# Attention heads: softmax denominators partly summed by GpSimd, value products in column quarters and in pairs, results kept channel-major in SBUF

## The chip, the cores and the metric

The kernel runs on one core of a Trainium2 chip. Its time is the device time of one execution in microseconds (us), taken as the median of several executions. The engines are named as in the profile: PE (TensorE), DVE (VectorE), ACT (ScalarE), POOL (GpSimd), SP (SyncE, which here only issues DMAs).

## The reference, cut to what matters

Four images of 256 channels and 32 x 32 pixels pass through an attention over pixels, a group norm with eight attention heads, and a mixture of eight experts. The change lies in the heads:

```python
qkv = (h @ w_qkv + b_qkv).reshape(B, N, H, 3, d)        # B=4, N=1024, H=8, d=32
q, k, v = (qkv[..., 0, :], qkv[..., 1, :], qkv[..., 2, :])
scores = jnp.einsum('bnhd,bmhd->bhnm', q, k) * (1.0 / np.sqrt(d)).astype(x.dtype)
attn = jax.nn.softmax(scores, axis=-1)
vals = jnp.einsum('bhnm,bmhd->bnhd', attn, v).reshape(B, N, C)
out = vals @ w_proj + b_proj
return out + x
```

All values are float32. There are 32 heads in all (4 images by 8), each with 1024 queries n and 1024 keys m.

## The kernel before, in words

The program has four phases, each a block at whose end all engines meet: `conv_phase` (first attention, group norm, projections of q, k and v), `head_phase` (the 32 heads), `output_phase` (projection of the heads' values, residual, layer norm, routing) and `expert_phase` (39 tiles of 128 tokens). Every instruction order is written out by hand, and semaphores tie the engines together.

**A head.** `head(t, j)` in `head_phase` handles head 4t + j in eight blocks i of 128 keys. Operands lie in a ring of four slots (`SLOTS`), loaded by SP with seven DMAs per head (`Heads.load`, L198 and L199). In a block PE does:

- `scores` (L946): two matmuls of 512 query columns into one of two pairs of PSUM banks, `ps_e`. ACT then writes their exponentials to SBUF (L928) as `expd`, a ring of four tiles of 128 x 1024.
- `maxima` (L209): q k once more, for a head one or two ahead and the other way round, queries on the partitions. DVE reduces each half of 512 to a maximum per query (`block_max`, L215). The two halves of `ps_m` are single buffers: PE may write a half only after DVE has read what was there, by the semaphore `v_max`. The maxima are `LEAD` = 12 blocks ahead of the scores.
- `values` (L962): for the exponentials of two blocks earlier, four matmuls that go to the four groups of 32 columns of the array at once: v and a matrix of ones, each for two halves of 512 queries. So a bank `ps_o` collects, over eight blocks, 32 rows of values and 32 rows of the same denominator, for each half of the queries.

After four blocks of a head the previous head is ended: ACT copies its bank to `osum` (L919), PE transposes that by four (L954), DVE takes the reciprocal of 8 denominators per partition (L1010) and multiplies (L1014), and SP stores 128 x 8 x 32 values to `o_scr` in DRAM (L869).

The maxima of the next head are made ready once per head: `split_max` on DVE (L225, L227, L229: a minimum, a cast and a difference of 128 x 8), `max_turn` on PE (L235, waits for `split_max`), `next_rows` on ACT (L242) and `max_rows` on SP (L248), which puts them as two rows into the scores' operand. Before, `split_max` follows the fourth block's maxima and `max_turn` the fifth block's values.

**Around it.** The first `LEAD` blocks of maxima are done at the end of `conv_phase`, between its last pieces of work, as the table `HEAD_BLOCKS` says: (2, 2, 2, 1, 1, 1, 1, 1, 1). Pieces 4 to 7 are the projections of q and k (`heads_qk`, L606: eight matmul instructions each, then ACT L476 and DVE L763, the latter ahead of the reductions of the block that follows the piece). POOL loads the experts' second weights `w2` during the heads (L910). At the end of `head_phase` SP loads constants, the values of image 0 and the residual. In `output_phase`, per image, the values are loaded from `o_scr` (`vals_load`), transposed on PE (`turn_vals`, L138), copied by ACT (L1130) and projected in two halves (`project`, L146); DVE adds the residual (L1240) and goes on from there.

```python
for half in range(2):
    for kind, w in enumerate((vh[s][:, m, :], ones[:, :])):
        c = (2 * half + kind) * D
        mm = nc.tensor.matmul(ps_o[k][c:c + D, :], w, expd[:, m % RING, half * HALF:(half + 1) * HALF], ...)
```

## Time and profile before

| what | value |
|---|---|
| median of 3 runs | 1323.39 us (1320.49 to 1324.12) |
| the profiled execution | 1324.85 us |
| its span, first to last instruction | 1323.0 us |
| mean granted TensorE clock | 0.95 of full speed |
| head phase, by the timeline | about 355.8 to 909.5 us |
| output phase | about 910 to 1000 us |
| expert phase | about 1000 to 1323 us |

The span is what the trace covers; the execution's own time is 1.85 us longer. In the trace PEld is the loading of weights into the array, which overlaps PE's matmuls, and L numbers are lines of the kernel before. In the changed kernel the same lines stand two to some twenty lines further on.

### The profile page before, as it was taken

How to read it: one execution, taken by the hardware profiler on the slowest of the kernel's cores; microseconds unless marked ns; L12 is line 12 of the kernel's file. 1: busy time of each engine (PE TensorE's matmuls, PEld its weight loads, DVE VectorE, ACT ScalarE, POOL GpSimd, SP SyncE). 2: the span in 40 equal slices, each digit the busy share in tenths (PEclk: the TensorE clock that was granted, in tenths of full speed). 3: DMA queues.
4: the chain of work that ended last, by engine and by line, in shares of the span. 5: the costliest groups of instructions: out<-in, count | busy, mean ns of one | idle time of the engine just before them, and what ended most of it. 6: DMA issues, size and time to landing. Idle time of an engine off the chain costs nothing. (4 is left out here: it accounts for less than half of the span.)

```text
span 1323.0 us, 21162 instructions
## 1 busy us (share of the span) xinstructions
PE 1219.5 (92%) x6723; PEld 772.7 (58%) x6724; DVE 682.5 (52%) x1540; ACT 420.2 (32%) x465; POOL 207.6 (16%) x418
## 2 busy tenths in 40 slices
PE   6899999895999999999999999998971999999995
PEld 3677676663534444444443444434861899999995
DVE  3265455446666666666666666652862333333331
ACT  1312132220255555555555555553210111111110
POOL 0002030302000000000000000000054244434442
PEclk8899999795999999999999999998965999999998
DMA  6203353131532332323323322205636565656551
GB/s 196 56 2 118 132 171 128 64 127 64 201 102 53 90 83 76 96 64 96 93 63 90 83 55 64 64 9 158 216 140 159 169 207 188 210 185 211 194 199 64
DMA packets 97141, 156.78 MB, mean 119 GB/s; under 512 B 44848, under 2 KB 65264, under 8 KB 96464
## 3 DMA queue, kind: packets, MB, share of 16 engines
q1 hardware_dynamic: 86576, 121.81, 30.1%
q0 software_dynamic: 9712, 31.35, 7.4%
q10 hardware_dynamic: 816, 3.15, 0.7%
q8 instruction: 21, 0.34, 0.1%
q14 instruction: 16, 0.13, 0.0%
HBM read 108.77 MB, written 44.06 MB: 116 GB/s over the span
## 5 line engine op out<-in xcount | busy, mean ns | idle before, releaser
L215 DVE TENSOR_REDUCE s_nmax<-h_ps_m 128x1 f32<-128x512 f32 x488 | 314.4, 686 | 178.2 <-PE h_ps_m L209 177.7
L928 ACT ACTIVATE h_expd<-h_ps_e 128x1024 f32<-128x1024 f32 x256 | 261.9, 1024 | 237.4 <-PE h_ps_e L946 232.6
L962 PE MATMUL h_ps_o<-h_expd,h_ones 128*32 128x512 f32 x1024 | 270.7, 604 | 0.0
L962 PE MATMUL h_ps_o<-h_expd,s_vh 128*32 128x512 f32 x1024 | 270.7, 604 | 0.0
L1559 PEld LDWEIGHTS ps_h<-xs_c,lnt 128*128 128x128 f32 x1248 | 148.2, 195 | 4.8 <-issue 2.9
L1559 PE MATMUL ps_h<-xs_c,lnt 128*128 128x128 f32 x1248 | 148.6, 278 | 2.3 <-DVE xs_c L1511 2.3
L1569 PE MATMUL ps_y<-w,vals_t 128*128 x624 | 141.2, 379 | 0.6 <-DVE ys L1524 0.6
L578 PE MATMUL a_ps_v<-a_val,a_expd 128*128 128x257 f32 x512 | 120.0, 388 | 5.1 <-ACT a_expd L456 4.5
L1569 PEld LDWEIGHTS ps_y<-w,vals_t 128*128 128x128 f32 x624 | 115.5, 190 | 15.1 <-issue 1.0
L1600 ACT ACTIVATE vals_t<-ps_h 128x1024 f32<-128x1024 f32 x39 | 39.9, 1024 | 263.3 <-DVE ps_h L1504 263.3
L1504 DVE TENSOR_TENSOR ps_h<-ps_h,b_t 128x1024 f32<-128x1024 f32 x39 | 48.1, 1233 | 131.5 <-PE ps_h L1559 131.5
L578 PEld LDWEIGHTS a_ps_v<-a_val,a_expd 128*128 128x128 f32 x512 | 98.0, 193 | 25.1 <-ACT a_expd L456 6.5
L962 PEld LDWEIGHTS h_ps_o<-h_expd,s_vh 128*32 128x32 f32 x1024 | 38.8, 108 | 93.6 <-issue 93.3
L687 DVE TENSOR_REDUCE a_nmax<-a_ps_m 128x1 f32<-128x512 f32 x64 | 41.2, 685 | 67.8 <-PE a_ps_m L538 67.8
L910 POOL DMA_DIRECT2D w<-in_w x8 | 7.1, 888 | 384.5 <-PE h_ps_e L946 384.5
L416 POOL TENSOR_TENSOR a_res<-a_res,a_lnt 128x2048 f32<-128x2048 f32 x4 | 18.1, 4532 | 265.2 <-DVE a_lnt L121 265.2
L606 PE MATMUL a_ps_e<-a_h_c,a_w_qk 128*128 128x512 f32 x128 | 58.6, 609 | 0.3 <-ACT a_h_c L467 0.3
L1401 POOL TENSOR_TENSOR pause<-pause 128x1 f32<-128x1 f32 x156 | 30.3, 194 | 158.6 <-DVE ys L1524 133.1
L946 PE MATMUL h_ps_e<-s_stk3n,s_stk3m 98*128 98x512 f32 x128 | 46.4, 444 | 0.0
L946 PE MATMUL h_ps_e<-s_stk1n,s_stk1m 98*128 98x512 f32 x128 | 46.4, 443 | 0.0
L946 PE MATMUL h_ps_e<-s_stk0n,s_stk0m 98*128 98x512 f32 x128 | 46.3, 443 | 0.0
L946 PE MATMUL h_ps_e<-s_stk2n,s_stk2m 98*128 98x512 f32 x128 | 46.3, 443 | 0.0
(188 smaller groups left out, 1421.9 us busy)
## 6 DMA issues: line engine op xcount, KB each, us to landing
lnt<-in_w SPq DMA_DIRECT2D x39, 1024.0 KB, 4.8
qk_scr<-a_head_hi SPq DMA_DIRECT2D x16, 512.0 KB, 2.7
qk_scr<-a_head_lo SPq DMA_DIRECT2D x16, 512.0 KB, 3.6
w<-in_w POOLq DMA_DIRECT2D x8, 1024.0 KB, 6.1
xs<-xs_scr SPq DMA_DIRECT2D x39, 128.5 KB, 2.0
a_x_t<-in_x_t POOLq DMA_DIRECT2D x4, 1024.0 KB, 10.4
r_scr<-a_res POOLq DMA_DIRECT2D x4, 1024.0 KB, 6.0
v_scr<-res SPq DMA_DIRECT2D x4, 1024.0 KB, 3.9
```

What stands on the lines that cost most here:

```text
L215: self.nc.vector.tensor_reduce(self.nmax[k][:, nb, half:half + 1], ps_m[:, half, :], AX.X, ALU.max, negate=True).then_inc(self.v_max, 1)
L578: last = nc.tensor.matmul(ps_v[:, j % 2, 0:C + 1], expd[:, m, j * P:(j + 1) * P], val[b % 2][:, m, :], start=(m == 0), stop=(m == NB - 1))
L606: last = nc.tensor.matmul(ps_e[it % 2][:, half, :], w_qk1[:, t, it, :], h_c[:, t, half * HALF:(half + 1) * HALF], start=(t == 0), stop=(t ...
L687: nc.vector.tensor_reduce(nmax[b % 2][:, nb, half:half + 1], ps_m[:, half, :], AX.X, ALU.max, negate=True).then_inc(v_max, 1)
L928: nc.scalar.activation(expd[:, m % RING, :], flat(ps_e[m % 2]), ACT.Exp, scale=SCALE).then_inc(a_exp, 1)
L946: last = nc.tensor.matmul(ps_e[m % 2][:, half, :], m_st[:, m * P:(m + 1) * P], n_st[:, half * HALF:(half + 1) * HALF], start=True, stop=True)
L962: mm = nc.tensor.matmul(ps_o[k][c:c + D, :], w, expd[:, m % RING, half * HALF:(half + 1) * HALF], start=(m == 0), stop=(m == NB - 1))
L1401: nc.gpsimd.tensor_tensor(pause[:, n:n + 1], pause[:, 0:1], pause[:, 0:1], ALU.add)
L1504: nc.vector.tensor_tensor(blocks, blocks, b1_t[:, bass.ds(e, 1), :].rearrange("p o (k n) -> p (o k) n", n=1).to_broadcast([P, KC, P]), ALU ...
L1559: last = nc.tensor.matmul(ps_h[k][:, c // 4, c % 4 * P:(c % 4 + 1) * P], w1_now[k][:, t, c * P:(c + 1) * P], xs_c[:, t, :], start=(t == 0) ...
L1569: last = nc.tensor.matmul(ps_y[:, 0:C], hid_t[k][:, c, :], w2[:, bass.ds(e, 1), c, :].rearrange("p o n -> p (o n)"), start=(c == 0), stop= ...
L1600: nc.scalar.activation(hid_t[k].rearrange("p k n -> p (k n)"), flat(ps_h[k]), ACT.Gelu).then_inc(a_gelu, 1)
```

## The change

1. **Values by query quarters** (`values`): all four column groups now hold v, each for a quarter of 256 queries. One tile of exponentials takes four matmuls of 256 columns in place of four of 512.
2. **Denominators** (`sums`, `all_sums`): into the other half of the same bank, ones times exponentials, by quarters as well. For tiles 6 and 7 of a head it is done directly; tiles 0 to 5 (`ADDED` = 6) are first added up by POOL, with five additions of 128 x 1024 per head, and PE multiplies only their sum. So a head has 8 + 3 rounds of four 256-column matmuls.
3. **Pairs** (`head` on PE): scores and maxima of two blocks follow each other, then the values of two earlier tiles; the last two tiles and their sums come in the first pair of the next head (`tail`).
4. **End of a head**: no copy by ACT and no transposes. DVE takes the reciprocal of a 128 x 256 tile of PSUM and multiplies 128 x 256. SP moves the result with four DMAs of 32 rows each into `vals`, which stays in SBUF with channels on the partitions.
5. **Lead**: the maxima are 14 blocks ahead; the table of `conv_phase` becomes (2, 2, 2, 2, 2, 1, 1, 1, 1). `split_max` now follows the second block's maxima, `max_turn` stands at the end of the first pair, and the slot of the head two ahead must be loaded by the third block in place of the fifth. `max_rows` goes ahead of the loads on SP.
6. **Buffers**: `expd` holds all eight tiles of a head. ACT waits for PE's values and POOL's additions of the head before.
7. **Loads**: `w2` is loaded by SP, one expert per four heads, from a host layout that is contiguous per partition; the constants and the first residual are loaded at the head phase's start.
8. **Output phase**: `vals_load`, `turn_vals` and ACT's copies (L1130) are gone; `project` reads `vals`.

```diff
-LEAD = NB + NB // 2
+LEAD = 2 * NB - 2
...
-HEAD_BLOCKS = (2, 2, 2, 1, 1, 1, 1, 1, 1)
+HEAD_BLOCKS = (2, 2, 2, 2, 2, 1, 1, 1, 1)
...
-        h = SLOTS * t + j
-        sp.wait_ge(v_norm, h + 1)
-        sp.dma_start(io["o_scr"][bass.ds(t + j // HG, 1), :, :, j % HG * D:(j % HG + 1) * D].rearrange("o p j d -> p (o j) d"),
-                     outh[j % 2][:, :, :]).then_inc(out_stored[j % 2], 16)
+        sp.wait_ge(v_norm, SLOTS * t + j + 2)
+        for q in range(4):
+            sp.dma_start(vals[j * D:(j + 1) * D, bass.ds(t, 1), q * QUARTER:(q + 1) * QUARTER].rearrange("p o c -> p (o c)"),
+                         outh[j % 2][q * D:(q + 1) * D, :]).then_inc(out_stored[j % 2], 16)
...
         h = SLOTS * t + j
+        if left >= 1:
+            hd.max_rows(sp, t, j + 1)
...
                 sp.wait_ge(pe_pv, NB * h)
                 hd.load(sp, io, t, j + SLOTS - 1)
             store(t, j - 1)
-        if left >= 1:
-            hd.max_rows(sp, t, j + 1)
+            if j == 2:
+                sp.dma_start(keep["w2"][:, bass.ds(t, 1)].rearrange("p o k m -> p (o k m)"),
+                             io["w2"][bass.ds(t, 1)].rearrange("o p m -> (o p) m")).then_inc(sems["w_in"], 16)
...
     sp.wait_ge(hd.v_stored, 16 * B)
-    stream(sp, head)
     for dst, src in consts:
         sp.dma_start(dst, src).then_inc(sems["consts_in"], 16)
-    vals_load(sp, io, keep, sems, 0)
     res_load(sp, io, keep, sems, 0)
+    stream(sp, head)
     store(HEADS // SLOTS - 1, SLOTS - 1)
...
-    for e in range(E):
-        pool.wait_ge(pe_exp, NB * (3 * e + 2))
-        pool.dma_start(keep["w2"][:, e], io["w2"][e].rearrange("(k p) m -> p k m", p=P)).then_inc(sems["w_in"], 16)
+    def head(t, j, first=False, left=SLOTS):
+        h, total = SLOTS * t + j, added[j % 2]
+        for m in range(1, ADDED):
+            pool.wait_ge(a_exp, NB * h + m + 1)
+            if m == 1:
+                if not first:
+                    pool.wait_ge(pe_sum, h)
+            else:
+                pool.wait_ge(g_add, (ADDED - 1) * h + m - 1)
+            nc.gpsimd.tensor_tensor(total[:, :], (expd[:, 0, :] if m == 1 else total[:, :]), expd[:, m, :],
+                                    ALU.add).then_inc(g_add, 1)
+    stream(pool, head)
...
-    def outputs(t, j):
-        h = SLOTS * t + j
-        act.wait_ge(pe_pv, NB * h + NB)
-        act.wait_ge(pe_ot, h + 1)
-        nc.scalar.activation(osum[:, :], ps_o[j % 2][:, :], ACT.Copy).then_inc(a_o, 1)
     def head(t, j, first=False, left=SLOTS):
         h = SLOTS * t + j
         for m in range(NB):
             act.wait_ge(pe_exp, NB * h + m + 1)
-            if not first or m >= RING:
-                act.wait_ge(pe_pv, NB * h + m - RING + 1)
-            nc.scalar.activation(expd[:, m % RING, :], flat(ps_e[m % 2]), ACT.Exp, scale=SCALE).then_inc(a_exp, 1)
-            if m == 1 and not first:
-                outputs(t, j - 1)
-            if m == 4 and left >= 1:
-                hd.next_rows(act, ps_o[(j + 1) % 2], t, j + 1)
+            if not first:
+                act.wait_ge(pe_pv, NB * (h - 1) + m + 1)
+                if m < ADDED:
+                    act.wait_ge(g_add, (ADDED - 1) * (h - 1) + max(m, 1))
+            nc.scalar.activation(expd[:, m, :], flat(ps_e[m % 2]), ACT.Exp, scale=SCALE).then_inc(a_exp, 1)
+            if m == 2 and left >= 1:
+                hd.next_rows(act, ps_o[j % 2], t, j + 1)
     stream(act, head)
-    outputs(HEADS // SLOTS - 1, SLOTS - 1)
...
-    def outputs(t, j):
-        pe.wait_ge(a_o, SLOTS * t + j + 1)
+    def values(j, m):
         for q in range(4):
-            last = nc.tensor.transpose(ps_o[j % 2][:, q * P:(q + 1) * P], osum[:, q * P:(q + 1) * P], ident[:, :])
-        last.then_inc(pe_ot, 1)
-    def values(s, k, m):
-        for half in range(2):
-            for kind, w in enumerate((vh[s][:, m, :], ones[:, :])):
-                c = (2 * half + kind) * D
-                mm = nc.tensor.matmul(ps_o[k][c:c + D, :], w, expd[:, m % RING, half * HALF:(half + 1) * HALF],
-                                      start=(m == 0), stop=(m == NB - 1))
-        mm.then_inc(pe_pv, 1)
+            mm = nc.tensor.matmul(ps_o[j % 2][q * D:(q + 1) * D, 0:QUARTER], vh[j % SLOTS][:, m, :],
+                                  expd[:, m, q * QUARTER:(q + 1) * QUARTER], start=(m == 0), stop=(m == NB - 1))
+        if m < ADDED:
+            mm.then_inc(pe_pv, 1)
+    def sums(j, e, done, last=False):
+        for q in range(4):
+            mm = nc.tensor.matmul(ps_o[j % 2][q * D:(q + 1) * D, QUARTER:2 * QUARTER], ones[:, :],
+                                  e[:, q * QUARTER:(q + 1) * QUARTER], start=False, stop=last, skip_group_check=True)
+        mm.then_inc(done, 1)
+    def tail(j):
+        for m in range(ADDED, NB):
+            values(j, m)
+        for m in range(ADDED, NB):
+            sums(j, expd[:, m, :], pe_pv)
+    def all_sums(t, j):
+        pe.wait_ge(g_add, (ADDED - 1) * (SLOTS * t + j + 1))
+        sums(j, added[j % 2], pe_sum, last=True)
+    def head(t, j, first=False, left=SLOTS):
+        h = SLOTS * t + j
+        for c in range(NB // 2):
+            for i in (2 * c, 2 * c + 1):
+                if i == 0:
+                    pe.wait_ge(*hd.loaded(maxrow_in, 32, t, j))
+                if not (first and i < 2):
+                    pe.wait_ge(a_exp, NB * h + i - 1)
+                scores(j % SLOTS, i)
+                ahead = 1 if i < 2 else 2
+                if left >= ahead:
+                    if i == 2:
+                        if first:
+                            pe.wait_ge(g_set, SLOTS - EARLY)
+                        pe.wait_ge(*hd.loaded(stack_in, 16 * STACK_DMAS, t, j + 2))
+                    hd.maxima(pe, ps_m, NB * h + LEAD + i, (j + ahead) % SLOTS, (i + LEAD) % NB)
+            if c == 0:
+                if not first:
+                    tail(j - 1)
+                    pe.wait_ge(v_norm, h)
+                if left >= 1:
+                    hd.max_turn(pe, ps_o[j % 2], ident, t, j + 1)
+            else:
+                if c == 1:
+                    if first:
+                        pe.wait_ge(out_stored[0], 16)
+                    if left >= 1:
+                        pe.wait_ge(hd.a_mrow, h + 2)
+                for m in (2 * c - 2, 2 * c - 1):
+                    values(j, m)
+                if c == 1 and not first:
+                    all_sums(t, j - 1)
+    stream(pe, head)
+    pe.wait_ge(a_exp, NB * HEADS)
+    tail(SLOTS - 1)
+    all_sums(HEADS // SLOTS - 1, SLOTS - 1)
...
+    nc.vector.memset(rc[:, :], 0.0).then_inc(v_norm, 1)
+    def norm(t, j):
+        h, got = SLOTS * t + j, ps_o[j % 2]
+        dve.wait_ge(pe_sum, h + 2)
+        dve.wait_ge(v_norm, h + 1)
+        nc.vector.reciprocal(rc[:, :], got[:, QUARTER:2 * QUARTER]).then_inc(v_rc, 1)
+        dve.wait_ge(v_rc, h + 1)
+        dve.wait_ge(out_stored[j % 2], 16 + 64 * (SLOTS // 2 * t + j // 2))
+        nc.vector.tensor_tensor(outh[j % 2][:, :], got[:, 0:QUARTER], rc[:, :], ALU.mult).then_inc(v_norm, 1)
...
-                if not first:
-                    norm(t, j - 1)
+                hd.block_max(dve, ps_m, NB * h + LEAD + i, (j + ahead) % 2, (i + LEAD) % NB)
+            if i == 1 and left >= 1:
+                hd.split_max(dve, t, j + 1)
+            if i == 4 and not first:
+                norm(t, j - 1)
...
-    def turn_vals(b):
-        pe.wait_ge(vals_in, 16 * b + 16)
+    def project(b, q):
+        if b == B - 1 and q == 0:
+            for k in range(2):
+                pe.wait_ge(sems[f"o_stored{k}"], 16 + 64 * B * NH // 2)
         if b:
-            pe.wait_ge(v_res1, 2 * b)
-        for t in range(CT):
-            turn(nc, ps_v[t], lambda j: vals_t[:, t, j, :], ident).then_inc(pe_vt, 1)
-    def project(b, q):
-        pe.wait_ge(a_vt, CT * b + CT)
-        by_token(nc, ps_v[q], vals_c, w_pr, q).then_inc(pe_pr, 1)
+            pe.wait_ge(v_res1, 2 * b + q - 1)
+        by_token(nc, ps_v[q], vals[:, b * CT:(b + 1) * CT, :], w_pr, q).then_inc(pe_pr, 1)
```

The instruction order of PE at the start of a head, in `head_phase` (`s_stk` operands, `h_ps_e` scores, `h_ps_m` maxima, `h_ps_o` the values' bank, `h_expd` exponentials). Before, a block:

```order
L946 MATMUL h_ps_e<-s_stk1n,s_stk1m 128x512 x2
L208 ISA
L209 MATMUL h_ps_m<-s_stk2m,s_stk2n 128x512 x2
L962 MATMUL h_ps_o<-h_expd,s_vh 32x512
L962 MATMUL h_ps_o<-h_expd,h_ones 32x512
L962 MATMUL h_ps_o<-h_expd,s_vh 32x512
L962 MATMUL h_ps_o<-h_expd,h_ones 32x512
L954 MATMUL h_ps_o<-ident,h_osum 128x128 x4
```

Now, the first pair of a head and the beginning of the second:

```order
L950 MATMUL h_ps_e<-s_stk3n,s_stk3m 128x512 x2
L210 ISA
L211 MATMUL h_ps_m<-s_stk0m,s_stk0n 128x512 x2
L950 MATMUL h_ps_e<-s_stk3n,s_stk3m 128x512 x2
L210 ISA
L211 MATMUL h_ps_m<-s_stk0m,s_stk0n 128x512 x2
L957 MATMUL h_ps_o<-h_expd,s_vh 32x256 x8
L965 MATMUL h_ps_o<-h_expd,h_ones 32x256 x8
L236 REGISTER_ALU
L237 MATMUL h_ps_o<-ident,s_msplit 16x128
L987 REGISTER_ALU
L950 MATMUL h_ps_e<-s_stk3n,s_stk3m 128x512 x2
```

Two blocks' maxima now stand a pair of scores apart, and the transpose of the split maxima (L237) stands ahead of the scores of the third block.

PE at the end of `conv_phase` (`a_ps_e<-a_h_c,a_w_qk` are the projections of q and k, `a_ps_m` the early maxima). Before:

```order
L606 MATMUL a_ps_e<-a_h_c,a_w_qk 128x512 x4
L209 MATMUL a_ps_m<-s_stk0m,s_stk0n 128x512 x2
L606 MATMUL a_ps_e<-a_h_c,a_w_qk 128x512 x4
L209 MATMUL a_ps_m<-s_stk0m,s_stk0n 128x512 x2
L606 MATMUL a_ps_e<-a_h_c,a_w_qk 128x512 x4
L209 MATMUL a_ps_m<-s_stk1m,s_stk1n 128x512 x2
```

Now:

```order
L608 MATMUL a_ps_e<-a_h_c,a_w_qk 128x512 x4
L211 MATMUL a_ps_m<-s_stk0m,s_stk0n 128x512 x4
L608 MATMUL a_ps_e<-a_h_c,a_w_qk 128x512 x4
L211 MATMUL a_ps_m<-s_stk1m,s_stk1n 128x512 x4
L608 MATMUL a_ps_e<-a_h_c,a_w_qk 128x512 x4
L211 MATMUL a_ps_m<-s_stk1m,s_stk1n 128x512 x2
```

After the first and after the second projection two blocks of maxima follow where one did.

DVE in a head of the changed kernel, around `split_max` (waits left out, `s_nmax` are the maxima):

```order
L217 TENSOR_REDUCE s_nmax<-h_ps_m 128x1
L227 TENSOR_TENSOR s_nmaxes<-s_nmax 128x8
L229 CAST s_msplit<-s_nmaxes 128x8
L231 TENSOR_TENSOR s_msplit<-s_nmaxes,s_msplit 128x8
L217 TENSOR_REDUCE s_nmax<-h_ps_m 128x1
L1030 RECIPROCAL h_rc<-h_ps_o 128x256
L1034 TENSOR_TENSOR outh<-h_ps_o,h_rc 128x256
```

The three small operations stand behind the fourth reduction of a head, which was the eighth; reciprocal and product stand behind the tenth.

## Rows read from the trace of the kernel before

**Rows 1.** The page: span, busy time, its shares, instructions

```profile
span 1323.0 us, 21162 instructions
...
PE 1219.5 (92%) x6723; PEld 772.7 (58%) x6724; DVE 682.5 (52%) x1540; ACT 420.2 (32%) x465; POOL 207.6 (16%) x418
```

**Rows 2.** Timeline, one block of a head: start, duration, engine, line, op, count [idle before]

```profile
651.88 0.73 PE L946 MATMUL h_ps_e<-s_stk1n,s_stk1m 98*128 98x512 f32 x2
...
652.72 1.02 ACT L928 ACTIVATE h_expd<-h_ps_e 128x1024 f32<-128x1024 f32 x1 [1.10 <-PE h_ps_e L946]
652.88 1.29 DVE L215 TENSOR_REDUCE s_nmax<-h_ps_m 128x1 f32<-128x512 f32 x2 [0.84 <-PE h_ps_m L209]
...
653.00 0.62 PE L962 MATMUL h_ps_o<-h_expd,s_vh 128*32 128x512 f32 x1
...
654.00 0.72 PE L946 MATMUL h_ps_e<-s_stk1n,s_stk1m 98*128 98x512 f32 x2
```

**Rows 3.** Timeline, last head, which has no maxima, and the phase's end

```profile
896.27 0.73 PE L946 MATMUL h_ps_e<-s_stk3n,s_stk3m 98*128 98x512 f32 x2
...
897.93 0.65 PE L954 MATMUL h_ps_o<-ident,h_osum 128*128 128x128 f32 x4
...
908.86 0.61 SPq L869 DMA_DIRECT2D o_scr<-outh  x1
...
913.86 4.63 PE L146 MATMUL c_ps_v<-w_pr,c_vals_c 128*128 128x256 f32 x10 [1.11 <-ACT c_vals_c L1130]
920.02 1.23 DVE L1240 TENSOR_TENSOR res<-c_ps_v,res 128x1024 f32<-128x1024 f32 x1 [11.19 <-PE c_ps_v L146]
```

**Rows 4.** Line L242, once per head: duration ns min/median/max, first and last start us

```profile
L242 ACT ACTIVATE s_mrow<-h_ps_o x31: 266/267/269, 365.5 to 886.6; 16x128 fp32r<-16x128 f32 x31
```

**Rows 5.** Timeline, the head phase's first blocks, where none multiplies values

```profile
356.89 3.86 DVE L215 TENSOR_REDUCE s_nmax<-h_ps_m 128x1 f32<-128x512 f32 x6 [1.37 <-PE h_ps_m L209]
...
357.63 0.19 PEld L209 LDWEIGHTS h_ps_m<-s_stk1m,s_stk1n 96*128 96x128 f32 x1 [0.52 <-DVE s_nmax L215]
...
358.23 0.19 PEld L209 LDWEIGHTS h_ps_m<-s_stk1m,s_stk1n 96*128 96x128 f32 x1 [0.41 <-DVE s_nmax L215]
```

**Rows 6.** Line L1010 and line L710, reciprocals out of PSUM, columns as in rows 4

```profile
L1010 DVE RECIPROCAL h_rc<-h_ps_o x32: 200/205/208, 380.9 to 908.2; 128x8 f32<-128x8 f32 x32
L710 DVE RECIPROCAL a_rc<-a_ps_v x32: 149/158/169, 61.4 to 294.8; 128x1 f32<-128x1 f32 x32
```

**Rows 7.** Groups by line: xcount, busy us, mean ns, idle before and releaser

```profile
L1014 DVE TENSOR_TENSOR outh<-h_ps_o,h_rc 128x256 f32<-128x256 f32 x32 | 13.6, 425 | 2.6
```

**Rows 8.** Line L416, the large POOL additions, columns as in rows 4

```profile
L416 POOL TENSOR_TENSOR a_res<-a_res,a_lnt x4: 4507/4537/4547, 96.9 to 308.7; 128x2048 f32<-128x2048 f32 x4
```

**Rows 9.** Timeline, DVE beside POOL's indirect DMA

```profile
968.69 0.97 POOL L1050 DMA_INDIRECT xs_scr<-lnt,pos  x1 [0.30 <-issue]
969.23 0.41 DVE L80 TENSOR_SCALAR c_rstd<-c_tmp 128x8 int32<-128x8 int32 x1
```

**Rows 10.** Lines L80 and L1271, small operations of SBUF alone, columns as in rows 4

```profile
L80 DVE TENSOR_SCALAR c_rstd<-c_tmp x4: 171/172/407, 927.1 to 969.2; 128x8 int32<-128x8 int32 x4
L1271 DVE CAST pos<-c_pos_f x4: 171/172/342, 961.1 to 994.1; 128x8 int32<-128x8 f32 x4
```

**Rows 11.** Timeline, end of the convolution phase

```profile
333.39 3.60 PE L606 MATMUL a_ps_e<-a_h_c,a_w_qk 128*128 128x512 f32 x8
...
335.48 1.28 DVE L215 TENSOR_REDUCE s_nmax<-a_ps_m 128x1 f32<-128x512 f32 x2
```

**Rows 12.** Line L199, the last load of a head's operands, columns as in rows 4

```profile
L199 SPq DMA_DIRECT2D s_vh<-v_scr x4: 352/390/426, 360.1 to 396.5; - x4
```

**Rows 13.** View of the DMA issues: xcount, KB each, median us to landing

```profile
s_vh<-v_scr SPq DMA_DIRECT2D x32, 128.0 KB, 2.5
o_scr<-outh SPq DMA_DIRECT2D x32, 128.0 KB, 2.7
```

**Rows 14.** Windows: length, busy us of PE, PEld, DVE, ACT, POOL (count), PEclk, DMA share, GB/s

```profile
920.00:930.00 10.00, 7.34 (x42) 6.20 (x41) 8.80 (x34) 1.94 (x2) 0.00 (x0) 1.00 0.46 141
```

More of the change, by code:

```diff
@@ L45 @@
 REGION = TB * P + P
+QUARTER = N // 4
+ADDED = 6
 STACK = 3 * D
@@ L968, in head @@
                     for i in range(NB):
-                        if i == 0:
-                            pe.wait_ge(*hd.loaded(maxrow_in, 32, t, j))
-                        if not (first and i < 2):
-                            pe.wait_ge(a_exp, NB * h + i - 1)
-                        scores(j % SLOTS, i)
-                        ahead = 1 if i < NB // 2 else 2
-                        if left >= ahead:
-                            if i == NB // 2:
-                                if first:
-                                    pe.wait_ge(g_set, SLOTS - EARLY)
-                                pe.wait_ge(*hd.loaded(stack_in, 16 * STACK_DMAS, t, j + 2))
-                            hd.maxima(pe, ps_m, NB * h + LEAD + i, (j + ahead) % SLOTS, (i + NB // 2) % NB)
```

100 lines of the change are left out of this document (20 added, 80 removed).

## The prediction

> **What bounds the kernel now.** The page comes first [rows 1]: PE is busy for 92% of the span, DVE for half, POOL for a sixth. That is an average over four phases, so the timeline of a block in the middle of the heads is next [rows 2]. From one block's scores to the next 654.00 − 651.88 = 2.12 us pass, and PE never idles, whereas ACT and DVE wait for it (1.10 and 0.84 us, the idle times in the brackets). Within the block the values take 654.00 − 653.00 = 1.00. In the last head, which has no maxima, a block takes 897.93 − 896.27 = 1.66 [rows 3], so maxima cost 2.12 − 1.66 = 0.46. The line that works once per head gives the period of a head [rows 4]: (886.6 − 365.5)/30 = 17.37 us, which is 8 × 2.12 plus 0.41 for the four transposes. The head phase is bound by PE, and 30 such periods are 521 of 1323 us.
>
> One limit is hidden. The first blocks of the phase have no values to multiply, and there PE waits for DVE [rows 5]: six halves are reduced in 3.86 us, 0.643 each. PE is let into the first half 357.63 − 356.89 = 0.74 after the reduction began, into the second 358.23 − 357.63 = 0.60 later. Today the values of a block cover this, as they stand between two blocks' maxima.
>
> **The change part by part, in the steady heads.** Of the 1.00 us for values I take 0.14 as entry and exit and 0.86 as streaming (four 512-column matmuls side by side); a round of 256 columns is then 0.43. Of the 2.12, scores and maxima stream for two times 0.425, so 2.12 − 0.86 − 0.85 = 0.41 goes to changes of operands. PE's own work falls. Per pair it has two blocks' scores and maxima (1.70), the changes (0.41, now once for two blocks) and two rounds (0.86): 2.97. A head is 4 × 2.97 plus three further rounds, 13.2 us; the four transposes (0.41) are gone. If nothing else counted, 4.2 us per head would be won.
>
> *Pairs.* But two blocks' maxima now follow each other with only a pair of scores between them, and a half of `ps_m` can't be written before DVE has read it. From the pair's start DVE begins after 652.88 − 651.88 = 1.00 [rows 2]. PE enters the second block's first half 0.74 later, its second half another 0.60 later, streams for 0.34, then does values with two switches (0.12 + 0.86 + 0.12). A pair is 1.00 + 0.74 + 0.60 + 0.34 + 1.10 = 3.78 us, and the head 4 × 3.78 plus 3 × 0.43 = 16.4. The pace is DVE's, not PE's.
>
> *Reciprocal.* It works on 128 x 256 out of PSUM. The trace has it only small: 158 ns for one element per partition, 205 for eight [rows 6]. That is 6.7 ns per further element, so 0.158 + 255 × 0.0067 = 1.87 us. The low bound is the product of 256 elements, 0.425 us [rows 7]; the high one takes the extremes of the same rows, (208 − 149)/7 = 8.4 ns, or 2.3 us. I take 1.87, as it is the same operation. With a wait of 0.15 and the product (0.42) DVE is held for 2.44 us between the reductions of blocks 4 and 5. In the pair DVE has 3.78 − 4 × 0.645 = 1.2 us to spare; the rest, 1.2 us, delays the fourth pair's maxima and with them PE. Head: 17.65 us. At the low bound nothing is delayed (16.4), at the high one 18.1.
> The Trainium skill, page "VectorE: DVE Perf Modes", section "Walkthrough: the 8-slice pipeline in each mode", calls the reciprocal an iterative divide that repeats eight times. Eight cycles of the 0.96 GHz engine per element would be about 2.1 us, an estimate from that page, and the sum below would become about 1385; the rows say 6.7 ns.
>
> *POOL's additions.* A 128 x 2048 addition takes 4.54 us [rows 8], so one of 1024 takes 2.3 and the five of a head 11.5. They fit into a period, so their own time costs nothing. Their place does. The first needs exponential 1. Exponential 0 starts 652.72 − 651.88 = 0.84 into a head [rows 2] and takes 1.02; the second ends at about 2.95, and POOL adds from 3.0 to 5.3. DVE reaches `split_max` after the fourth reduction, at 1.00 + 0.74 + 0.60 + 0.34 + 0.25 + 0.65 = 3.6: in the middle of that addition. Its three operations work on SBUF alone. The trace shows what such ones do beside POOL: a shift of 128 x 8 begun at 969.23 ends at 969.64, and POOL's indirect DMA, begun at 968.69, at 969.66 [rows 9]. The same line takes 171 ns otherwise and 407 here, and line L1271 goes from 171 to 342 [rows 10]. They look blocked till POOL's instruction is done. So `split_max` would be through not at 4.2 but at 5.3 + 0.6 = 5.9, while PE, after its second block (2.7), a switch and the four rounds of the tail (1.7), is at `max_turn` by 4.5: it waits some 1.3 us in each head. The later additions can't hit it, and reductions, reciprocal and product read PSUM. Head: 17.65 + 1.3 = **18.9 us**. Bounds: 0 (no blocking) and 2.3 (a whole addition).
> The Trainium skill, page "SBUF — State Buffer", section "Who interferes with whom", names an exclusive port pair of DVE and GpSimd, for which the second to come is fully blocked; it speaks of DVE instructions with two SBUF inputs or in a two-port mode. By that rule too `split_max` waits; rows 9 agree with it for an instruction of one source.
>
> **The ends.** *Steady heads:* 30 × (18.94 − 17.37) = +47. *Convolution's end:* two extra blocks of maxima stand right behind a first block. Such a block waits for reductions which stand behind DVE's work on the projection; a projection is 3.60 and DVE reduces the maxima before it at 335.48, 2.1 into it [rows 11]. I charge each extra block one projection, 2 × 3.65 = +7.5 (bounds 2 × 0.46 by PE's work alone, and 8). *Head phase's start:* the last load for slot 2 is issued at 360.1 and lands 2.5 later or, behind its neighbours, 3.1 [rows 12, 13]; the third block now needs it instead of the fifth, at about 360.2: +3 (0 to 4). *Last two heads:* hardly any maxima, so a block is not held by DVE but the five additions chain: before 15.5 + 16.4, after 13 + 18.3: −0.6 (±3). *Output phase:* from the store at 908.86 to DVE's first sum at 920.02 there are 11.2 us [rows 3]; now four stores at 0.61 (2.4 with their overlap, landing in SBUF at a store's 2.7 [rows 13]), the meeting of the engines and the projection's 6.2 (913.86 to 920.02): −3 (−5 to 0). Gone with `turn_vals` is only PE and ACT time, hidden beside DVE, which is busy for 8.80 of 10 us there [rows 14]; this cover stays. *At nothing:* the loads of `w2` (SP idles in the heads, the transfers are over long before the experts), `max_rows` ahead of the loads, ACT's waits (exponential m waits for additions a head old, done at about 3 + 11.5 us while tile 5 comes up for use after 18.9 + 9). *Clock:* PE would work 13.2 of 18.9 us. It was granted 1.00 at 7.34 busy of 10 [rows 14], so I charge nothing.
>
> Sum: 47 − 0.6 + 3 + 7.5 − 3 = +54. Against the profiled execution, 1324.85, that is 1379; against the median, 1.5 lower, **1377 us**.
>
> **Rivals.** *B, POOL disturbs nothing.* For it: only single-source operations, and only DMAs of POOL, were seen together; the addition is another kind of instruction. Head 17.65: 30 × 0.28 + 7 = +15, about 1339. The same comes out if the reciprocal is fast but blocking stays (17.7 us, 1341).
> *C, faster: DVE's added operations cost what L1014 costs, whatever the operation and whoever works beside it.* Then norm is 0.425 + 0.15 + 0.42 = 1.0 us between blocks 4 and 5, inside the 1.2 to spare, and `split_max` is done by 4.2, before PE asks for it. Head 16.4: 30 × (−0.97) + 7 = −22, about 1302. It decides from a norm of 1.2 us on, above which each us of it is a us of the head. Against it speak rows 6, whose slope is four times that of L1014, and rows 9.
> *D, dearer: more small instructions, or a longer reciprocal.* At 8.4 ns per element the head is 19.4 us, about 1391. The same if the 44 matmuls of 256 columns come out at 0.5 us a round: 11 × 0.07 = 0.8 us, of which the three extra rounds and those on the waiting path show.
> *E, balance:* pairs hidden by ACT's and DVE's slack so that a head takes 17.1: within 0.3% (4 us, what a measurement of this kernel can tell from none). It would need half of each charge.
>
> **How the numbers follow.** Forecast 0.56; B with its twin 0.18; C 0.10; D 0.12; E 0.04. The predicted time is the forecast's. The forecast alone spans 1360 to 1392 (blocking 0.8 to 1.8 us, ends ±6). To leave out no more than 2 in 10 I take B in and most of D: 1330 to 1398, without C, E and D's upper end. Slower by over 0.3%: forecast, D and most of B, 0.84; within: 0.05; faster: C and an edge of E, 0.11.
>
> **What would show it.** The line of `next_rows`, once per head, gives the period: 18.9 (B 17.65, C 16.4). The reciprocal's own row: 1.87 us. PE's wait before the transpose in `max_turn`, some 1.3 us, put down to DVE; and the middle of `split_max`'s first operation lasting till an addition of POOL ends. Between two maxima of a pair PE idles for DVE. PE's busy share of the head phase falls to 70%. In the convolution's last pieces PE waits twice for reductions. Wrong it would be if the reciprocal took under a microsecond, if the additions of POOL took over 3.4 us each (then POOL, at 17 and more per head, sets the pace), or if DVE's small operations kept 0.17 us beside them.

## The result and the profile after

The changed kernel takes **1391.05 us** (1390.34 to 1392.29, 4 runs) against 1323.76 (4 runs of the kernel before): ratio 1.051, 95% interval 1.049 to 1.053. It is slower, by 67 us. The forecast was 1377, its range 1330 to 1398. The profiled execution has a span of 1389.2 us, 66.2 more than that of before.

The page of the changed kernel, span and parts 1 and 2, beside [rows 1]:

```profile
span 1389.2 us, 23073 instructions
...
PE 1203.8 (87%) x7299; PEld 818.7 (59%) x7300; DVE 775.4 (56%) x1541; ACT 380.5 (27%) x425; POOL 582.9 (42%) x570
...
PEclk8999999886899999999999999999775799999998
```

PE is busy for less time than before (1204 us after 1220) in a longer span, and the granted clock falls short in more slices: 0.923 in the mean against 0.95.

Where the 66.2 us lie is read from a few starts. The head phase begins at 365.5 (before: 355.8), and its PE work ends before the output phase's first matmul at 974.6 (910.3); DVE's first residual sum is at 981.5 (920.0). The forecasts in the last column are the terms of the prediction's sum; its term for the output phase is counted from the last head's first store on, which lies in the row above it.

| stretch | before | after | difference | forecast |
|---|---|---|---|---|
| up to the head phase | 355.8 | 365.5 | +9.7 | +7.5 |
| 30 heads, by the line of `next_rows` | 521.1 | 573.2 | +52.1 | +47 |
| the rest of the head phase | 33.4 | 35.9 | +2.5 | +2.4 |
| to DVE's first residual sum | 9.7 | 6.9 | −2.8 | −3 |
| from there to the end | 403.0 | 407.7 | +4.7 | 0 |

The line that works once per head (columns as in [rows 4]), and by the timeline three of its instructions that follow each other:

```profile
L244 ACT ACTIVATE s_mrow<-h_ps_o x31: 248/250/252, 372.4 to 945.6; 16x128 fp32r<-16x128 f32 x31
```

```profile
679.78 0.25 ACT L244 ACTIVATE s_mrow<-h_ps_o 16x128 fp32r<-16x128 f32 x1
...
699.87 0.25 ACT L244 ACTIVATE s_mrow<-h_ps_o 16x128 fp32r<-16x128 f32 x1
...
718.29 0.25 ACT L244 ACTIVATE s_mrow<-h_ps_o 16x128 fp32r<-16x128 f32 x1
```

The mean period is (945.6 − 372.4)/30 = 19.11 us, but no head has it. One lasts 20.09, the next 18.42. Over the phase 18 of the 30 distances are 18.25 to 18.54 us, and 12 are 19.85 to 21.5 (a long head, from here on). Before, all lay between 16.9 and 17.5.

**An undisturbed head.** The timeline of its first pair, from the second block's maxima on:

```profile
713.51 1.07 PE L957 MATMUL h_ps_o<-h_expd,s_vh 128*32 128x256 f32 x16
713.60 2.37 POOL L919 TENSOR_TENSOR h_added<-h_expd 128x1024 f32<-128x1024 f32 x1 [3.72 <-ACT h_expd L935]
...
714.34 1.65 DVE L227 TENSOR_TENSOR s_nmaxes<-s_nmax 128x8 f32<-128x8 f32 x1
714.39 1.05 PE L965 MATMUL h_ps_o<-h_expd,h_ones 128*32 128x256 f32 x16
716.02 0.17 DVE L229 CAST s_msplit<-s_nmaxes 128x8 fp32r<-128x8 f32 x1
716.23 0.17 DVE L231 TENSOR_TENSOR s_msplit<-s_nmaxes,s_msplit 128x8 fp32r<-128x8 f32 x1
716.45 0.09 PEld L237 LDWEIGHTS h_ps_o<-ident,s_msplit 128*16 128x16 f32 x1 [1.49 <-DVE s_msplit L231]
```

`split_max`'s first operation, 8 elements wide, takes 1.65 us and ends at 715.99; POOL's addition, begun 0.74 before it, ends at 715.97. As soon as it is over, DVE's two next operations take 0.17 each. PE waits meanwhile.

How long PE waits depends on the row that one reads. The loading of weights (PEld) has 1.49 here, as it runs ahead of the matmuls; by PE's own rows the array stands idle for 0.9 to 1.2 us before this transpose.

The end of a head on DVE, in the third and fourth pair, by the timeline:

```profile
722.95 1.75 DVE L1030 RECIPROCAL h_rc<-h_ps_o 128x256 f32<-128x256 f32 x1
...
724.73 0.42 DVE L1034 TENSOR_TENSOR outh<-h_ps_o,h_rc 128x256 f32<-128x256 f32 x1
725.07 2.56 DVE L217 TENSOR_REDUCE s_nmax<-h_ps_m 128x1 f32<-128x512 f32 x4
...
725.81 0.19 PEld L211 LDWEIGHTS h_ps_m<-s_stk0m,s_stk0n 96*128 96x128 f32 x1 [1.00 <-DVE s_nmax L217]
```

The last row is the second long wait of PE, here called the one behind the reciprocal: 1.0 to 1.1 us by the loads of weights, 0.6 to 0.7 by PE's own rows. The fourth pair takes 4.6 to 4.7 us by it where the clock holds.

**A long head.** The windows of the changed kernel (columns as in [rows 14]) around the slow stretch of the head whose period runs from 659.78 to 679.78:

```profile
667.00:669.00 2.00, 1.51 (x5) 0.86 (x5) 2.00 (x4) 0.79 (x1) 1.92 (x2) 1.00 0.12 31
669.00:671.00 2.00, 1.92 (x18) 0.69 (x17) 1.52 (x3) 1.02 (x1) 0.78 (x1) 0.77 0.14 35
671.00:673.00 2.00, 2.00 (x8) 1.42 (x5) 0.03 (x1) 0.37 (x1) 0.00 (x0) 0.50 0.00 0
673.00:675.00 2.00, 1.90 (x11) 0.93 (x14) 2.00 (x4) 1.67 (x2) 0.00 (x0) 0.88 0.00 0
```

The seventh value is the granted clock. After the wait behind the reciprocal it drops from 1.00 to 0.50, the lower of the two levels (1.2 of 2.4 GHz), and is back some three microseconds later; from 671 to 673 PE is busy throughout, it is just slow. Each of the 12 long heads has such a stretch, the one of 21.5 us has two, and no short head has one. In the first of them it begins at 366.3, at the start of the head phase and ahead of both waits; in the others it begins 2.0 to 2.7 us behind the end of one of the two, four times of that for the split maxima and eight times of that behind the reciprocal.

### The profile page after: what moved, and what is told of

Read it like the earlier page. It is cut to its first block and busy times, and to the rows that moved or that the text cites. A ratio compares the mean times of both kernels' runs of the same rounds, so it can differ in the third digit from the quotient of the medians.

```text
span 1389.2 us, 23073 instructions
## 1 busy us (share of the span) xinstructions
PE 1203.8 (87%) x7299; PEld 818.7 (59%) x7300; DVE 775.4 (56%) x1541; ACT 380.5 (27%) x425; POOL 582.9 (42%) x570
## 5 line engine op out<-in xcount | busy, mean ns | idle before, releaser
L919 POOL TENSOR_TENSOR h_added<-h_added,h_expd 128x1024 f32<-128x1024 f32 x128 | 303.8, 2373 | 90.3 <-ACT h_expd L935 82.1
L957 PE MATMUL h_ps_o<-h_expd,s_vh 128*32 128x256 f32 x2048 | 147.2, 408 | 1.2 <-ACT s_mrow L244 0.8
L1555 PE MATMUL ps_y<-w,vals 128*128 x624 | 141.2, 379 | 0.6 <-DVE ys L1510 0.6
L919 POOL TENSOR_TENSOR h_added<-h_expd 128x1024 f32<-128x1024 f32 x32 | 75.8, 2368 | 126.3 <-ACT h_expd L935 126.3
L1555 PEld LDWEIGHTS ps_y<-w,vals 128*128 128x128 f32 x624 | 115.5, 190 | 15.1 <-issue 1.0
L1586 ACT ACTIVATE vals<-ps_h 128x1024 f32<-128x1024 f32 x39 | 40.0, 1025 | 260.3 <-DVE ps_h L1490 260.3
L1030 DVE RECIPROCAL h_rc<-h_ps_o 128x256 f32<-128x256 f32 x32 | 56.0, 1749 | 21.1 <-PE h_ps_o L965 21.1
L211 PE MATMUL h_ps_m<-s_stk2m,s_stk2n 96*128 96x512 f32 x128 | 55.3, 465 | 10.9 <-DVE s_nmax L217 3.9
L211 PE MATMUL h_ps_m<-s_stk3m,s_stk3n 96*128 96x512 f32 x128 | 54.5, 456 | 11.0 <-DVE s_nmax L217 5.2
L211 PE MATMUL h_ps_m<-s_stk1m,s_stk1n 96*128 96x512 f32 x116 | 50.6, 470 | 9.6 <-DVE s_nmax L217 4.7
```

The lines of the kernel that those rows point to most:

```text
L211: self.nc.tensor.matmul(ps_m[:, half, :], n_st[0:STACK, nb * P:(nb + 1) * P], m_st[0:STACK, half * HALF:(half + 1) * HALF], start=True, st ...
L919: nc.gpsimd.tensor_tensor(total[:, :], (expd[:, 0, :] if m == 1 else total[:, :]), expd[:, m, :], ALU.add).then_inc(g_add, 1)
L957: mm = nc.tensor.matmul(ps_o[j % 2][q * D:(q + 1) * D, 0:QUARTER], vh[j % SLOTS][:, m, :], expd[:, m, q * QUARTER:(q + 1) * QUARTER], star ...
L1030: nc.vector.reciprocal(rc[:, :], got[:, QUARTER:2 * QUARTER]).then_inc(v_rc, 1)
L1555: last = nc.tensor.matmul(ps_y[:, 0:C], hid_t[k][:, c, :], w2[:, bass.ds(e, 1), c, :].rearrange("p o n -> p (o n)"), start=(c == 0), stop= ...
```

## Experiments

Periods below are those of the line of `next_rows`, computed as above from the first and last start of its 31 instructions in the profiled execution; L numbers are each kernel's own. All times are medians; the kernel before, measured beside each, took 1323.5 to 1324.6. The first head is long in every run, in the one-pair version by little (16.5): a slow stretch begins there at the start of the phase, ahead of the waits in question; "long heads" below count it.

### POOL after the split

```diff
 if m == 1:
+    if left >= 1:
+        pool.wait_ge(hd.v_split, h + 2)
     if not first:
```

> POOL's first addition of a head now also waits for split_max of the next head (v_split), so none of POOL's additions can run while DVE does the three small SBUF operations. Theory (POOL's addition blocks them; the first took 1.64 us in the median where it takes 0.17 otherwise): all three take 0.17, PE's wait of about 1.2 us before the transpose of the split maxima goes, the undisturbed head falls from 18.45 to about 17.2 us, the kernel by 30 x 1.24 = 37 us to about 1354. If the stretches of low granted clock inside the heads (about 1.5 us in 13 of 30 heads) come from PE's waits, many of them go too: down to 1335. Rival 1 (the long operation is DVE's own, POOL has no part): nothing moves, 1391. Rival 2 (POOL's later start makes its chain the limit): the sums of a head come late and PE waits for POOL in the second pair; no gain or a loss.

Measured 1344.8 us (1343.5 to 1346.3), 46 less than the changed kernel; period 17.55. The line of the operation that took 1.64 us in the median:

```profile
L227 DVE TENSOR_TENSOR s_nmaxes<-s_nmax x32: 166/167/169, 338.1 to 897.9; 128x8 f32<-128x8 f32 x32
```

Not one of the 32 is long, since none stands beside an addition. The same operation, the same engine, only POOL's start moved: the blocking is shown. The undisturbed head is 17.29 us, 1.15 less; long heads are down to 5 of 30 (the expectation speaks of 13 before; by the count they are 12), so some low clock went with the wait. The four besides the first all have their slow stretch behind the reciprocal.

### No reciprocal

```diff
-nc.vector.reciprocal(rc[:, :], got[:, QUARTER:2 * QUARTER])
+nc.vector.tensor_copy(rc[:, :], got[:, QUARTER:2 * QUARTER])
```

> The reciprocal is replaced by a copy of the same 128 x 256 tile (values then come out multiplied by the denominator instead of divided). Theory (DVE is held 2.20 us between blocks 4 and 5 where the pair has 1.2 to spare): the copy takes about 0.42 us in place of 1.75, the fourth pair falls from 4.72 to 3.77 us, the undisturbed head to 17.5, the kernel by 28 us to about 1363, more if stretches of low clock go with the wait. Rival (DVE's hold is absorbed elsewhere, the pace is set by the chain of the first pair): less than 10 us.

This kernel leaves out the division, so it only prices the operation. Measured 1354.9 us (1352.6 to 1357.1), 36 less; undisturbed head 17.55, 0.9 less, and 6 long ones of 30. The five besides the first all have their slow stretch behind the wait for the split maxima, the one that is left.

### Both edits

> Both edits. Theory: the terms add, since they lie in different pairs: head 16.3 us, which is the price of the pairs alone (4 x 3.77 and three rounds of 0.43), and no stretch of low clock left in the heads: 1391 - 66 - 20 = about 1305, faster than the kernel before. If the low clock comes from pairing itself (PE waits 0.5 and 0.4 us in each pair for DVE) and not from the two long waits, it stays and the time is about 1325.

The division is left out here too. Measured 1312.9 us (1311.3 to 1314.8); ratio to the kernel before 0.992 (0.990 to 0.995). Apart from the first (19.4), every head is 16.3 to 16.5 us. So the two terms add (46 + 36 = 82 against 78), 16.4 us is the price of the pairs, and PE's short waits for DVE within a pair don't bring the clock down: it is 1.00 from 378 to the heads' end. These waits are 0.52 and 0.41 us by the loads of weights and at most 0.11 by PE's own rows. The 1305 were missed by 8.

### Single blocks

```diff
-for c in range(NB // 2):
-    for i in (2 * c, 2 * c + 1):
+for i in range(NB):
...
-        if c == 0:
-            if not first:
-                tail(j - 1)
+    if i < 2:
+        if not first:
+            values(j - 1, ADDED + i)
+            sums(j - 1, expd[:, ADDED + i, :], pe_pv)
...
-            for m in (2 * c - 2, 2 * c - 1):
-                values(j, m)
+        values(j, i - 2)
```

> With the first edit (POOL after the split), and PE's order by single blocks: scores, maxima and one tile's values (in the first two blocks of a head one tile's values and its sums), then the next block. Theory (the pairs make DVE the pace, 3.77 us a pair where PE alone needs 2.97): by single blocks a block is 1.70 us by PE's own work and DVE's 1.29 fits in; the head is 8 x 1.70 + 3 x 0.43 = 14.9, plus about 1.6 for the reciprocal and product and 0.8 for the split, 17.3 us. So it comes out level with the run that has the first edit alone, with the wait for DVE concentrated at the two places, about 1354. Rival (pairs are what the change gains by): 4 more entries and exits of grouped mode, 0.25 each, on top of the DVE waits: 18.3 us, about 1385.

A clear miss: 1449.9 us (1445.4 to 1451.6). The timeline shows blocks of 1.69 us where nothing is waited for, as reckoned, but also three waits that single blocks lay bare, since nothing longer stands ahead of them, and after them heads of 21 us with low clock:

```profile
646.03 0.09 PEld L237 LDWEIGHTS h_ps_o<-ident,s_msplit 128*16 128x16 f32 x1 [1.32 <-DVE s_msplit L231]
...
648.26 0.64 PE L959 MATMUL h_ps_o<-h_expd,s_vh 128*32 128x256 f32 x8 [0.94 <-ACT s_mrow L244]
...
656.13 1.10 PE L211 MATMUL h_ps_m<-s_stk3m,s_stk3n 96*128 96x512 f32 x2 [1.05 <-DVE s_nmax L217]
```

The reckoning had left out the second: values of tile 0 go into the bank in which the transposed maxima still wait for ACT. So this run leaves open what pairs are worth; the last runs by single blocks below answer it.

### The end of a head in parts

```diff
-if i == 4 and not first:
-    norm(t, j - 1)
+if i in (3, 5, 7) and not first:
+    norm(t, j - 1, (i - 3) // 2)
```

Part 0 is the reciprocal of 128 columns, part 1 that of the other 128, part 2 the product.

> The first edit (POOL after the split), and the end of a head cut in three on DVE: the reciprocal of 128 columns behind block 3's reductions, of the other 128 behind block 5's, the product behind block 7's, where DVE sits idle 1.1 to 1.7 us before the next pair's first reduction. Nothing of the computation is left out. Theory (only the part of the reciprocal that doesn't fit into such a gap costs): a piece takes about 0.16 + 127 x 0.0062 = 0.95 us and fits, the head comes to the 16.4 us of the run without reciprocal, the kernel to about 1314, 30 us less than with the first edit alone and 10 less than the kernel before. Rival (the first piece comes too late, since it waits for the sums that PE multiplies at the end of the second pair, and delays the third pair): half of the gain, about 1330.

Measured 1314.8 us (1313.6 to 1316.6), ratio 0.994 (0.992 to 0.995): the whole computation in the time of the run without reciprocal. The line of the reciprocal:

```profile
L1034 DVE RECIPROCAL h_rc<-h_ps_o x64: 895/952/959, 396.4 to 894.5; 128x128 f32<-128x128 f32 x64
```

DVE works 0.16 us more on it than in one piece (2 × 0.952 against 1.749), and the kernel loses nothing by it.

### Early blocks earlier

```diff
-HEAD_BLOCKS = (2, 2, 2, 2, 2, 1, 1, 1, 1)
+HEAD_BLOCKS = (2, 2, 4, 1, 1, 1, 1, 1, 1)
```

> As the run before, and the two added blocks of early maxima moved from behind the first two q and k projections into the stretch before them: HEAD_BLOCKS (2, 2, 4, 1, 1, 1, 1, 1, 1). Theory (each cost 4.05 us, 3.1 of it PE's wait for reductions that stand behind the projection's own DVE work, and then a stretch of low clock): the projections run without such a wait; the blocks cost about 2.3 us where they stand now, so 6 to 7 us are won, about 1307. Rival (the low clock, which is there before and after, sets this stretch): 3 us.

Measured 1305.0 us (1304.2 to 1307.7), 9.8 less than the run before it. In the profiled executions the head phase begins 5.6 us earlier (361.0 against 366.6), which is nearer to the 6 to 7 expected. The next run, whose kernel is the same up to there, has 355.6: executions of one kernel differ in this part by several microseconds, by how long the granted clock was 0.50 (68 us in the one, 58 in the other), and a few of the +9.7 us can be that. In the changed kernel the timeline at this place had

```profile
336.21 2.56 DVE L217 TENSOR_REDUCE s_nmax<-a_ps_m 128x1 f32<-128x512 f32 x4
336.95 0.19 PEld L211 LDWEIGHTS a_ps_m<-s_stk0m,s_stk0n 96*128 96x128 f32 x1 [3.09 <-DVE s_nmax L217]
...
345.54 5.29 PE L608 MATMUL a_ps_e<-a_h_c,a_w_qk 128*128 128x512 f32 x8
```

twice such a wait of 3.1 us (the other at 344.60), and then a projection that took 5.29 us where the rows of before have 3.60 [rows 11], at the lower clock.

### More work for PE in the output phase

```diff
+if b and q == 0:
+    by_token(nc, ps_v[q], vals[:, b * CT:(b + 1) * CT, :], w_pr, q)
 by_token(nc, ps_v[q], vals[:, b * CT:(b + 1) * CT, :], w_pr, q).then_inc(pe_pr, 1)
```

> As the run before, and in the output phase the first half of each later projection is done twice (the same result), in place of the transposes that the change took out, so that PE idles less between the first images. Theory (with the transposes gone PE idles 5.1 us before the first layer norm's result and is then granted half the clock, so DVE waits 4.2 and 2.4 us for the projections): the clock stays, DVE's waits shrink, the phase loses 3 to 5 us. Rival (the doubled work itself delays DVE): 2 to 4 us slower.

Measured 1308.5 us (1305.2 to 1311.1). From DVE's first residual sum to the end the profiles give 409.3 us here and 405.7 without the doubled work. That is the rival's case, though the ranges of the two runs overlap; the forecast gain of 3 to 5 us isn't there. The +4.7 us of the last stretch stays unexplained by a run. What the profile of the changed kernel shows there is that DVE waits for the projections in 6 places (19.1 us; before 15.2 in 4). The first of them, 10.0 and before 11.2 us, belongs to the stretch ahead, so within this one it is 9.1 us after 4.0. The windows from 990 to 1010 have a clock of 0.66 and 0.73 where before, some 61 us earlier, had 1.00.

### PE works through its waits

```diff
 pe.wait_ge(v_norm, h)
+for _ in range(10):
+    nc.tensor.transpose(ps_o[j % 2][:, 0:P], ident[:, :], ident[:, :])
```

> The changed kernel with one addition: ten transposes of the identity into the bank that the transpose of the split maxima overwrites, right ahead of it, where PE now waits some 1.2 us for DVE. The waits for DVE stay as long; PE only works instead of idling. Theory (the 13 of 30 heads with 1.5 us more are heads whose granted clock fell because PE idled): the long heads become rare, the undisturbed period stays 18.45, about 1391 - 15 = 1376. Rival (the low clock has another cause): 1391, or some 5 to 10 us more where the filler outlasts the wait.

Inconclusive in its time: 1389.3 us, but from 1378.9 to 1394.3; the profiled execution was the fastest, with 7 long heads of 30 (the next expectation says 8). The second wait, behind the reciprocal, was still there, and this profile says more than the time: the six long heads besides the first all have their slow stretch behind that wait, none behind the filled one. So both were filled, with the scores of block 6 repeated as well:

```diff
+if i == 6 and not first:
+    for _ in range(2):
+        scores(j % SLOTS, i, False)
 scores(j % SLOTS, i)
```

> The changed kernel with PE's two long waits filled by repeated work: the ten transposes ahead of the transpose of the split maxima, and the scores of block 6 computed three times over (the same result), where PE then waits for the reductions behind the reciprocal. DVE's and POOL's order is that of the changed kernel. Theory (the heads of 19.9 us are those after which the granted clock fell because PE idled; with one of the waits filled 8 of 30 were left in the profiled execution): hardly a long head is left, nearly all at 18.4 to 18.6 us, 1365 to 1375. Rival (low clock has another cause than PE's idling, or the filling only moves the wait): 1380 to 1400, with long heads as before.

Measured 1374.9 us (1372.9 to 1378.8), 16 less than the changed kernel, by nothing but superfluous work of PE. One long head is left, the first; the others are 18.40 to 18.66. The line of `next_rows`:

```profile
L244 ACT ACTIVATE s_mrow<-h_ps_o x31: 248/250/251, 372.8 to 929.8; 16x128 fp32r<-16x128 f32 x31
```

That is 18.57 us a head against 19.11, and (19.11 − 18.57) × 30 = 16 us. DVE waits and works as before, and only PE no longer stands idle: the long heads come from PE's idling.

### One pair

Single blocks once more, as in the run with early blocks moved, now with each of the three waits taken away:

```diff
-if i == 1:
+if i == 2:
     pe.wait_ge(v_norm, h)
     hd.max_turn(pe, ps_o[j % 2], ident, t, j + 1)
...
-values(j, i - 2)
+if i == 3:
+    pe.wait_ge(hd.a_mrow, h + 2)
+    values(j, 0)
+if i >= 3:
+    values(j, i - 2)
...
-if m == 2 and left >= 1:
+if m == 1 and left >= 1:
     hd.next_rows(act, ps_o[j % 2], t, j + 1)
...
-if i in (3, 5, 7) and not first:
-    norm(t, j - 1, (i - 3) // 2)
+if i >= 3 and not first:
+    norm(t, j - 1, i - 3)
```

The parts of the last edit are four reciprocals of 64 columns and the product.

> A whole version, nothing of the computation left out: as the run with early blocks moved, but PE goes by single blocks and only blocks 2 and 3 form a pair; the transpose of the split maxima stands behind block 2's maxima, its copy by ACT behind exponential 1; DVE takes the reciprocal in four pieces of 64 columns behind blocks 3 to 6 and the product behind block 7. Theory (the run by single blocks had blocks of 1.69 us wherever nothing was waited for; it lost its time to three waits, for the split maxima 0.84, for the maximum rows 0.94, for the reciprocal 1.05 us, and to the low clock that followed): those waits are taken away here, a head is 8 x 1.70 + 3 x 0.43 = 14.9, plus some 0.4 for the pair and 0.6 for the pieces, 15.9 us; the kernel 0.5 us a head less than the 1305 us of the best so far, about 1290. Rival (single blocks bring the low clock whatever the waits): heads of 17 to 21 us in the mixture, 1330 or more.

Measured **1272.8 us** (1268.8 to 1275.2, 6 runs); ratio to the kernel before 0.962 (0.959 to 0.964). It beats both kernels, and the 1290 expected by 17. The timeline of a block in the middle of a head:

```profile
649.55 0.73 PE L952 MATMUL h_ps_e<-s_stk2n,s_stk2m 98*128 98x512 f32 x2
...
650.06 0.55 DVE L1037 RECIPROCAL h_rc<-h_ps_o 128x64 f32<-128x64 f32 x1
...
650.55 1.29 DVE L217 TENSOR_REDUCE s_nmax<-h_ps_m 128x1 f32<-128x512 f32 x2
...
651.24 0.73 PE L952 MATMUL h_ps_e<-s_stk2n,s_stk2m 98*128 98x512 f32 x2
```

The block is 651.24 − 649.55 = 1.69 us, a head 15.29 (15.9 were expected; the pieces of 0.55 us fall into DVE's gaps, and PE's own rows show no wait in the heads).

> The same without the pair: all blocks single, the transpose of the split maxima still behind block 1, the reciprocal in four pieces. Theory: the wait for the reciprocal is gone (-1.5 us against the 18.4 us of an undisturbed head of the first run by single blocks), the waits for the split (0.84) and for the rows (under 0.94, as ACT's copy comes earlier) stay: 16.5 to 16.9 us where the clock holds, about 1310 to 1320. Rival (low clock comes with single blocks): the long heads of 21 us remain, 1380 or more.

Without the pair, the transpose behind block 1 as at first: 1294.3 us (1294.1 to 1297.8), below the 1310 expected at least; undisturbed head 15.8, below the expected 16.5 to 16.9, and no long head but the first (27.0). So single blocks don't bring the low clock, and that of the first run by single blocks went with its waits. But one of the three is still there, by the groups of PE (columns as in [rows 7]):

```profile
L237 PE MATMUL h_ps_o<-ident,s_msplit 128*16 128x128 f32 x31 | 8.7, 280 | 25.0 <-DVE s_msplit L231 25.0
```

These are 0.8 us of idle PE once in each head, and the granted clock is 1.00 from 389 to 873 all the same. In the first experiment 0.6 us once in each head, in pairs, went with four slow stretches. So the length of a wait alone doesn't decide; what else does, no run here shows.

### All sums on PE

```diff
-if m < ADDED:
-    mm.then_inc(pe_pv, 1)
+sums(j, expd[:, m, :], pe_pv, last=(m == NB - 1))
```

> The one-pair version without POOL's part: PE multiplies ones with every tile's exponentials (8 rounds of sums in place of 3), POOL adds nothing, DVE's small operations stand beside no addition. Theory (PE is the bound there, 15.25 us a head, all of it work): five more rounds of 0.43 us each, 2.15 us a head, 17.4 us, as much as the kernel before; the kernel 30 x 2.15 = 65 us more than the 1272.8, about 1337. Rival (POOL's additions cost the others something that the run's order hides badly, ports or DMA): under 40 us more.

Measured 1338.8 us (1337.8 to 1341.5), 66 more than the one-pair version; period 17.47, or 2.18 more. What POOL takes off PE is worth just its five rounds. That is also what the new layout wins over the old within a head, as far as these orders show: with all sums on PE a head takes about what it took before (17.37).

## Why the prediction was right, and where it was not

- **Pairs.** 3.78 us were worked out from rows of before; the third pair of a head takes 3.77 in the changed kernel, and the head without the two other costs 16.4, as forecast.
- **Reciprocal.** 1.75 us measured, 1.87 forecast from the slope of two small ones; the product 0.42 as said. The delay is 0.9 us a head, not 1.2: the fourth pair takes 4.6 to 4.7 where 3.77 + 1.2 was reckoned. The estimate from the Trainium skill, page "VectorE: DVE Perf Modes", section "Walkthrough: the 8-slice pipeline in each mode", 2.1 us, was further off than the slope of the rows.
- **POOL's additions.** The place, the operation hit and its end (with POOL's) were as forecast. Without the blocking a head is 1.15 us shorter, where 1.3 were charged (the prediction's own figures, 5.9 − 4.5, give 1.4); the additions take 2.37 each. The rule of the Trainium skill, page "SBUF — State Buffer", section "Who interferes with whom", agrees with this trace: the later instruction is blocked till the earlier one ends (1.65 us where it takes 0.17 alone), and it has two SBUF inputs.
- **The undisturbed head** is thus 18.45 us, 0.5 below the forecast; 30 × (18.45 − 17.37) = 32 us of the steady term, where 47 were reckoned.
- **Clock: the step that failed.** The prediction charged nothing, because PE had been granted 1.00 at 7.34 busy of 10 us [rows 14]. In the changed kernel 12 of 30 heads carry a stretch at 0.50, 1.5 us and more each: 573.2 − 30 × 18.45 = 20 us. The term for these two waits held their length only; what the runs showed in place of nothing is that PE's idling in them also lowers the granted clock behind them in about two heads of five. A mean of busy time over 10 us said nothing of that. The run with both waits filled gives 16 of the 20 back. The two misses, −15 and +20, hide each other in the total, so the forecast of +54 stands nearer to +67 than its steps deserve.
- **PE's share.** The sign that PE would be busy for 70% of the head phase didn't come: from 384 to 938 it is 485.6 of 554 us, 88%. The rows of PE count part of its waiting as busy: two matmuls of maxima last 0.63 us in the first block of a pair and 1.10 in the second, where the second half is waited for. So this share can't judge the 13.2 us of own work; that a block without waits takes 1.69 us in the one-pair version, of which 0.43 are values, bears out the terms for scores, maxima and changes of operands.
- **Convolution's end.** From one projection to the next 7.66 us pass where an added block lies between (345.54 − 337.88), and 3.9 before: 3.75 per added block, close to the 3.65 charged (the 4.05 of the expectation took off the projection alone). What was missing is 1.7 of low clock behind them and 0.6 by which this kernel was late before it (ACT's `a_h_c` at 325.80, before 325.17): +9.7, forecast 7.5. Moving the two blocks won 9.8 by the medians, 5.6 by the profiled executions at this place.
- **Output phase.** The table's −2.8 against −3 is in part luck. Counted as the forecast was, from the last head's first store to DVE's first sum, it is 981.52 − 971.51 = 10.01 us after 11.16, only −1.15; and from the phase's start to that store, less the 30 periods, +0.9, where head phase's start and last two heads were given +2.4. The two errors cancel. "This cover stays" did not come true: +4.7 us later in the phase. The removal of the transposes as a cause was argued from the clock there and not confirmed by the run that added work.
- **Rivals.** The time of rival B (1339) is about what the first experiment reaches (1344.8), but only once the blocking is taken away. Rival C's 16.4 us a head came true, but only after both of its conditions were made: by another place for POOL and by a reciprocal in parts.

## What to carry to other kernels

When an edit lets two stages that hand a single buffer back and forth stand closer together, reckon the loop of the two engines, not the busy time of the busier one: it gave the pair to 0.01 us. A long operation on the engine that is nearly the pace goes in pieces into the gaps it has anyway, and a small SBUF operation is put where no GpSimd addition can be under way. And a recurring wait of TensorE can cost more than its length: here two waits of about half a microsecond to one microsecond in each head brought 1.5 us more in two heads of five, while in another order one of 0.8 us brought nothing, so look at the granted clock behind it. The same work in an order in which PE hardly waits turned a loss of 5% into a gain of 4%.

## Not expected of the hardware

- The granted clock fell to 0.50 for some three microseconds, 2.0 to 2.7 us behind two waits of a head, 0.9 to 1.2 and 0.6 to 0.7 us by PE's own rows (1.4 to 1.7 and 1.0 to 1.1 by the loads of weights). It did so in 11 heads besides the first; with one of the two waits gone in 4 or 5, all behind the other; with work in both in none. In the run with both edits, and in single blocks with one wait of 0.8 us a head, it was 1.00 from the second head on.
- DVE's reciprocal out of PSUM is linear in its width: 0.55 us for 64 elements per partition, 0.95 for 128, 1.75 for 256, about 6.2 ns for each.
- POOL's addition of two SBUF tiles holds DVE's small operation to its own end (715.97 and 715.99), while reductions, reciprocal and product out of PSUM beside POOL's additions kept their times: 1.29 for two reductions, 1.75, 0.42.
